# Moving the two halves of a split copy to other places in a software pipeline

## The chip, the core and the metric

The kernel runs on one core of a Trainium2 chip. The metric is device time in microseconds, the median of the runs shown. The engines named here are TensorE (PE in profiles, PEld for its weight loads), VectorE (DVE), ScalarE (ACT), GpSimd (POOL) and SyncE (SP, here the issuer of DMAs). Each works through its own queue in order, and semaphores tie them together.

## The reference

Four sequences of 1024 tokens with 128 features pass through an attention layer and a mixture-of-experts layer, each with a layer norm before, one behind and a residual. The change touches attention alone:

```python
q = (hidden_states @ Wq).reshape(b, s, H, D).transpose(0, 2, 1, 3)     # H 16, D 64
k = (hidden_states @ Wk).reshape(b, s, HKV, D).transpose(0, 2, 1, 3)   # HKV 4
v = (hidden_states @ Wv).reshape(b, s, HKV, D).transpose(0, 2, 1, 3)
q = _apply_rope(q, cos, sin)
k = _apply_rope(k, cos, sin)
scores = jnp.einsum('bkgqd,bkpd->bkgqp', qg, k) * scale
scores = jnp.where(causal, scores, jnp.float32(-1e+30))
probs = jax.nn.softmax(scores, axis=-1)
out = jnp.einsum('bkgqp,bkpd->bkgqd', probs, v)
```

## The kernel before, in words

Attention is one software pipeline of 128 steps: 4 batches (b), 4 key-value heads each (a "group", g), 8 steps a group (s, `STEPS_G`). A step treats two heads that share the partitions, and two tiles of 128 query rows: a big one, whose causal row has 1024, 896, 768 or 640 keys (steps 0 to 3, and again 4 to 7 for the second pair of heads), and a small one with 128, 256, 384 or 512 keys. The steps 2 to 7 of one group and 0 to 1 of the next stand in a hardware loop; the first two steps and the last six of a batch are written out.

Scores are made from operands in two parts, high and low, as q_high·k_high + q_low·k_high + q_high·k_low. Six "rope" tiles (k = 0 to 5, 128 x 512) supply them for each group: 0 and 1 are keys, 2 and 3 the queries of the first pair, 4 and 5 those of the second. `project_step(k)` says in which step a tile is projected: 0 to 3 in steps 3 to 6 of the group before, 4 and 5 in steps 0 and 1 of the group itself. A tile then passes through these stations:

- TensorE projects it into `proj_bank` at the end of its step; ScalarE's `keep_raw` (line 695) copies it to `raw`.
- SyncE's `swap_pairs` (line 315) moves neighbouring partitions of `raw` to `turned` with two DMAs.
- In the next step GpSimd multiplies `raw` by the cosines (line 927, after its own `spread_sums`, line 916), `turned` by the sines (line 907), and adds both into `roped` (line 932).
- In that next step too, ScalarE's `keep_high` (line 704) copies `roped` as float32r to the high tile, and VectorE's `rope_work(.., "low", ..)` (line 1038) subtracts that from `roped` into the low tile.

So a high copy is due in steps 4, 5, 6, 7, 1 and 2. The order of a step on each engine is fixed by the program:

- TensorE (`step`): big score rows (line 422, first the keys from 512 on, then the lower 512), which need the small exponentials of the step before for the lower part alone; three groups of transposes ("turns", line 441) of the last step's probabilities; the outputs of the step before that (line 471); small score rows, which need this step's big exponentials; two more groups of turns (441, 447); the projection.
- ScalarE (`step`): copy of the turned group 0 (line 725), two big exponentials (716), the high copy, two small exponentials, copy of the turned group 4, and `keep_raw`. At the end of a batch (`last`, s = 2) `keep_tokens` takes the next batch's tokens, at its start (s = 1) `keep_out` the projected output.
- VectorE (`attend`): reciprocal of the last step's sums (line 1052), two big maxima (1046), copies of the turned groups 1 and 2 (1060), the scaled output (1074), two small maxima, the turned group 3, the subtraction. In some steps of the first and last group parts of a layer norm follow (`next_norm`, `out_norm`).

GpSimd's spread waits for the reciprocal of the same step. Score rows wait for the low tiles (`rope_low`): big rows of step 0 for tile 2, small ones of step 0 for tile 3, big ones of step 4 for tile 5.

Of the kernel before, what the change touches and what calls it, by code (L numbers as in the profile page):

```python
# [13 lines left out]
B, S, HID = 4, 1024, 128  # L14
# [11 lines left out]
PROJ_A, PROJ_B = 4, 2  # L26
ROPES_G = PROJ_A + PROJ_B
ROPES_B = ROPES_G * HKV
STEPS_P = TILES // 2
STEPS_G = PAIRS * STEPS_P  # L30
# [14 lines left out]
def rope_index(b, g, k):  # L45

    return b * ROPES_B + g * ROPES_G + k


def step_index(b, g, s):  # L50

    return b * STEPS_B + g * STEPS_G + s


def widths(n):

    return n + 1, TILES - n
# [23 lines left out]
def half_of(k):  # L81

    return (0, 1, 1, 0, 1, 0)[k]


def project_step(k):

    return 3 + k if k < PROJ_A else k - PROJ_A
# [7 lines left out]
def rope_plan(b, s, lag, last):  # L96

    out = []
    for k in range(ROPES_G):
        if project_step(k) + lag == s and not (last and b == B - 1 and k < PROJ_A):  # L100
            out.append((1 if k < PROJ_A else 0, k))
    return out


def build(nc, io, out):
    with ExitStack() as ctx:
# [3 lines left out]
        def bank(name):  # L110
            return ctx.enter_context(nc.psum_tensor(name, [128, HALF], F32))
# [73 lines left out]
        o_out, proj_bank = bank("o_out"), bank("proj_bank")  # L185
# [47 lines left out]
        def earlier(g, s, lag):  # L233

            return (g, s - lag) if s >= lag else (g - 1, s - lag + STEPS_G)
# [130 lines left out]
        def _(pe):  # L366
# [108 lines left out]
            def step(b, g, s, last, depth):  # L475
# [29 lines left out]
                for ahead, k in rope_plan(b, s, 0, last):  # L505
                    project(b, g + ahead, k, proj_bank)
# [177 lines left out]
        def _(act):  # L684
# [12 lines left out]
            def keep_high(b, g, k):  # L697

                cols = slice(half_of(k) * HALF, half_of(k) * HALF + HALF)
                act.wait_ge(rope_sum, rope_index(b, g, k) + 1 + ROPES_G)  # L700
                if k < 2:
                    act.wait_ge(k_copied, 32 * (b * HKV + g + 1))
                dst = kk[0] if k < 2 else qh[0 if k < PROJ_A else 1]
                A(dst[:, cols], roped[:, k % 2, :], ACT.Copy).then_inc(rope_high, 1)  # L704

            def exponentials(b, g, s, big):

                n = s % STEPS_P
                sigma = step_index(b, g, s)
                width = widths(n)[big] * 128  # L710
                if big:
                    act.wait_ge(turn_full, MOVES * sigma + MOVES)
                for h in range(2):
                    item, q = (0 if big else 2) + h, block_at(n, big, h)
                    act.wait_ge(max_ready, 4 * sigma + item + 1)
                    A(probs[:, s % 2, q * 128:q * 128 + width], rows[h][:, 0:width], ACT.Exp,  # L716
                      bias=neg_max[:, s % 2, item:item + 1], accum_out=exp_sum[:, s % 2, item:item + 1]).then_inc(exp_done, 1)

            def keep_turned(b, g, s, j):

                sigma = step_index(b, g, s)
                first = moves(s % STEPS_P)[j][0]
                act.wait_ge(turn_full, MOVES * sigma + j + 1 + 2 * MOVES)
                act.wait_ge(pv_done, sigma + 1)
                A(probsT[:, s % 2, first * 128:first * 128 + HALF], ring[j % 3][:, :], ACT.Copy  # L725
                  ).then_inc(kept_act, 1)
# [8 lines left out]
            def keep_tokens(b, a, src):  # L735

                act.wait_ge(x_turned, 2 * b + a + 1)
                if b < B:
                    A(xT[:, 0, a * HALF:a * HALF + HALF], src[:, :], ACT.Copy).then_inc(x_high, 1)
                else:  # L740
                    A(x2T[a], src[:, :], ACT.Copy).then_inc(x2_kept, 1)

            def keep_out(b, a, src):

                act.wait_ge(wo_done, 2 * b + a + 1)
                if a == 0 and b:
                    act.wait_ge(mid_done, b)
                A(attn_out[:, 4 * a:4 * a + 4, :].rearrange("p t d -> p (t d)"), src[:, :], ACT.Copy).then_inc(wo_kept, 1)  # L748
# [8 lines left out]
            def step(b, g, s, last, depth):  # L757

                at = earlier(g, s, 1)
                first = isinstance(g, int) and g == 0  # L760
                if depth > 0:
                    keep_turned(b, *at, 0)
                exponentials(b, g, s, 1)
                for ahead, k in rope_plan(b, s, 1, last):
                    keep_high(b, g + ahead, k)
                if last and s == 2:
                    keep_tokens(b + 1, 0, proj_bank)
                if first and s == 1:
                    inverse_deviations(2 * b if b else 1, 0, TILES)
                if last and s == 4 and b:  # L770
                    inverse_deviations(2 * b + 1, TILES, 2 * TILES)
                exponentials(b, g, s, 0)
                if depth > 0:
                    keep_turned(b, *at, 4)
                if last and s == 2:
                    keep_tokens(b + 1, 1, proj_bank)
                if first and s == 1 and b:
                    keep_out(b - 1, 0, proj_bank)
                    keep_out(b - 1, 1, o_out)
                for ahead, k in rope_plan(b, s, 0, last):  # L780
                    keep_raw(b, g + ahead, k, proj_bank)
                if first and s == 0 and b:
                    keep_values(b)
# [157 lines left out]
        def _(dve):  # L941
# [80 lines left out]
            def rope_work(b, g, stage, k):  # L1022
                r, c = rope_index(b, g, k), k % 2
                cols = slice(half_of(k) * HALF, half_of(k) * HALF + HALF)
                if stage == "cos":
                    dve.wait_ge(rope_low, r + 1)
                    dve.wait_ge(raw_kept, r + 1)
                    V.tensor_tensor(roped[:, c, :], raw[:, k % 4, :], cf[:, C_COS + half_of(k) * HALF:C_COS + half_of(k) * HALF + HALF],
                                    ALU.mult).then_inc(cos_done, 1)
                elif stage == "sum":  # L1030
                    dve.wait_ge(cos_done, r + 1)
                    dve.wait_ge(sin_done, r + 1)
                    V.tensor_tensor(roped[:, c, :], roped[:, c, :], turned[:, c, :], ALU.add).then_inc(rope_sum, 1)
                else:
                    p = 0 if k < PROJ_A else 1
                    high, low = (kk[0], kl[0]) if k < 2 else (qh[p], ql[p])
                    dve.wait_ge(rope_high, r + 1)
                    V.tensor_tensor(low[:, cols], roped[:, c, :], high[:, cols], ALU.subtract).then_inc(rope_low, 1)

            def row_maxima(b, g, s, big):  # L1040

                width = widths(s % STEPS_P)[big] * 128
                for h in range(2):
                    item = (0 if big else 2) + h
                    dve.wait_ge(rows_full, 4 * step_index(b, g, s) + item + 1)
                    V.tensor_reduce(neg_max[:, s % 2, item:item + 1], rows[h][:, 0:width], AX_X, ALU.max, negate=True  # L1046
                                    ).then_inc(max_ready, 1)

            def invert_sums(b, g, s):

                dve.wait_ge(exp_done, 4 * step_index(b, g, s) + 8)
                V.reciprocal(inv_sum[:, s % 2, :], exp_sum[:, s % 2, :]).then_inc(sum_inverted, 1)  # L1052
# [23 lines left out]
            def attend(b, g, s, last, depth):  # L1076

                g1, s1 = earlier(g, s, 1)
                if depth > 0:
                    invert_sums(b, g1, s1)  # L1080
                row_maxima(b, g, s, 1)
                if depth > 0:
                    keep_turned(b, g1, s1, 1)
                    keep_turned(b, g1, s1, 2)
                if depth > 1:
                    keep_outputs(b, *earlier(g, s, 2))
                if last and s == 2 and b + 1 < B:
                    split_tokens(b + 1, 0, proj_bank)
                row_maxima(b, g, s, 0)
                if depth > 0:  # L1090
                    keep_turned(b, g1, s1, 3)
                for ahead, k in rope_plan(b, s, 1, last):
                    rope_work(b, g + ahead, "low", k)
                if last and s == 2 and b + 1 < B:
                    split_tokens(b + 1, 1, proj_bank)
                if isinstance(g, int) and g == 0 and s < 2:
                    next_norm(b, s)
                if last and b:
                    out_norm(b, s)
# [206 lines left out]
```

## Time and profile before

| | us |
|---|---|
| median of 3 runs | 1491.96 |
| lowest and highest | 1490.4, 1493.01 |
| the profiled execution | 1484.45 |
| its span, first to last instruction | 1482.4 |
| attention pipeline in it, roughly | 50 to 1156 |
| busy: TensorE, VectorE, ScalarE, GpSimd | 1333.7, 981.0, 774.2, 407.7 |

Busy time is a sum over stages. A matmul's end is modelled and overlaps the next one's start, so that a busy TensorE isn't one at its peak. Idle time is named in brackets with the instruction that ended it. An ordinary group of eight steps takes 63.8 us, and the groups at the ends of a batch take longer.

### The profile page before, as it was taken

Reading aid. Unit: us, or ns where it says so; the run is one execution under the profiler, and the core shown is the slowest. Engines: PE = TensorE matmul, PEld = TensorE weight load, DVE = VectorE, ACT = ScalarE, POOL = GpSimd, SP = SyncE. Lnnn points to the kernel's source line nnn. Section 1 sums busy time; section 2 is a strip of 40 time slices with the busy share of each in tenths; the row PEclk is TensorE's granted clock in tenths of the full one; section 3 lists DMA queues with packets and bytes.
Section 4 is the critical chain, followed back from the end, with each engine's and each line's share of the span. In section 5 each row is a group of like instructions: output and inputs, shape, how many; then the busy total and the mean of one; then the engine's idle time right before and its main releaser. Section 6 shows DMA issues by size and latency. Waiting matters only on the chain.

```text
span 1482.4 us, 31001 instructions
## 1 busy us (share of the span) xinstructions
PE 1333.7 (90%) x10417; PEld 931.1 (63%) x10432; DVE 981.0 (66%) x2044; ACT 774.2 (52%) x1709; POOL 407.7 (27%) x412
## 2 busy tenths in 40 slices
PE   2699999899999988998999989999999899999996
PEld 1477677677676766876766668676766644444442
DVE  3677777664777768476777775777768257666665
ACT  2556666554566556365566554666665233333333
POOL 0343444322434424143434331434440000000000
PEclk9799999999999999999999999999999999999999
DMA  8211112110111110112111111111110000000000
GB/s 235 82 38 64 60 46 67 38 58 28 64 53 67 35 61 29 58 41 69 35 67 57 43 54 33 55 50 67 49 57 2 1 1 8 7 8 8 8 8 14
DMA packets 79028, 67.64 MB, mean 46 GB/s; under 512 B 39904, under 2 KB 62304, under 8 KB 78816
## 3 DMA queue, kind: packets, MB, share of 16 engines
q1 hardware_dynamic: 78944, 66.55, 13.8%
q8 instruction: 49, 0.80, 0.2%
q14 instruction: 35, 0.29, 0.1%
HBM read 7.81 MB, written 2.10 MB: 7 GB/s over the span
## 4 chain that ended last, share of the span: by engine, by line
PE 36%; POOL 14%; ACT 14%; DMA 12%; issue 10%; DVE 7%; SPq 4%; ACTq 1%; POOLq 0%; DVEq 0%
DMA turned<-raw 12%; POOL turned L907 7%; POOL roped L932 7%; PE rows L611 7%; ACT probs L716 7%; PE rows L422 6%; PE o_out L471 5%; PE o_out L634 3%; PE turn L441 3%; ACT raw L695 3%; SPq L315 3%; ACT probsT L725 2%; DVE neg_max L1046 2%; PE o_out L390 2%; PE proj_bank L390 1%
## 5 line engine op out<-in xcount | busy, mean ns | idle before, releaser
L1046 DVE TENSOR_REDUCE neg_max<-rows 128x1 f32<-128x768 f32 (+7 forms) x512 | 363.7, 752 | 226.6 <-PE rows L425 226.6
L716 ACT ACTIVATE probs<-rows,neg_max 128x768 f32<-128x768 f32 (+7 forms) x512 | 373.2, 734 | 89.3 <-DVE neg_max L1046 86.2
L471 PE MATMUL o_out<-probsT,v_g 128*64 128x128 f32 (+1 forms) x3328 | 278.5, 318 | 0.7 <-DVE probsT L1060 0.7
L471 PEld LDWEIGHTS o_out<-probsT,v_g 128*64 128x64 f32 x3328 | 201.5, 137 | 68.5 <-issue 19.6
L441 PE MATMUL turn<-cf,probs 128*128 128x128 f32 x1792 | 242.8, 276 | 1.3 <-DVE probsT L1060 1.1
L422 PE MATMUL rows<-kk,qh 64*128 64x512 f32 (+2 forms) x768 | 170.8, 441 | 80.7 <-ACT probs L716 74.6
L725 ACT ACTIVATE probsT<-turn 128x512 f32<-128x512 f32 x256 | 152.5, 596 | 142.2 <-PE turn L441 138.4
L441 PEld LDWEIGHTS turn<-cf,probs 128*128 128x128 f32 x1792 | 195.1, 143 | 1.9 <-DVE probsT L1060 1.3
L916 POOL COPY inv_wide<-inv_sum 128x256 f32<-128x256 f32 x128 | 50.9, 398 | 507.3 <-DVE inv_sum L1052 476.5
L422 PEld LDWEIGHTS rows<-kk,qh 64*128 64x128 f32 x768 | 72.4, 185 | 168.2 <-ACT probs L716 120.3
L1060 DVE COPY probsT<-turn 128x512 f32<-128x512 f32 x256 | 174.5, 682 | 1.5 <-PE turn L441 1.1
L907 POOL TENSOR_TENSOR turned<-turned,cf 128x512 f32<-128x512 f32 x96 | 122.7, 1279 | 166.8 <-DMA turned<-raw 166.8
L611 PE MATMUL rows<-roped,w_exp 128*128 128x512 f32 x320 | 154.4, 606 | 1.1 <-ACT attn_out L748 0.7
L422 PE MATMUL rows<-kk,ql 64*128 64x512 f32 (+2 forms) x768 | 135.3, 348 | 0.0
L422 PE MATMUL rows<-kl,qh 64*128 64x512 f32 (+2 forms) x768 | 135.3, 347 | 0.0
L927 POOL TENSOR_TENSOR roped<-raw,cf 128x512 f32<-128x512 f32 x92 | 117.2, 1274 | 55.3 <-ACT raw L695 55.2
L932 POOL TENSOR_TENSOR roped<-roped,turned 128x512 f32<-128x512 f32 x92 | 117.2, 1274 | 13.3
L1174 DVE TENSOR_TENSOR probs<-rows,probs 128x512 f32<-128x512 f32 x80 | 55.1, 688 | 90.7 <-PE o_out L634 76.1
L704 ACT ACTIVATE qh<-roped 128x512 fp32r<-128x512 f32 x64 | 40.4, 631 | 133.7 <-POOL roped L932 132.4
L860 ACT ACTIVATE probs<-rows 128x512 f32<-128x512 f32 x80 | 47.8, 597 | 102.5 <-PE rows L611 102.4
L716 ACT ACTIVATION_READ_ACCUMULATOR probs<-rows,neg_max 128x1 f32 x512 | 100.9, 197 | 0.0
L611 PEld LDWEIGHTS rows<-roped,w_exp 128*128 128x128 f32 x320 | 59.9, 193 | 64.5 <-issue 58.7
(154 smaller groups left out, 1677.8 us busy)
## 6 DMA issues: line engine op xcount, KB each, us to landing
turned<-raw SPq DMA_DIRECT2D x192, 128.0 KB, 2.0
kk<-kk SPq DMA_DIRECT2D x16, 512.0 KB, 2.9
kl<-kl SPq DMA_DIRECT2D x16, 512.0 KB, 3.7
v_g<-v_all SPq DMA_DIRECT2D x32, 256.0 KB, 3.0
slab_a<-w_qk SPq DMA_DIRECT2D x16, 256.0 KB, 2.6
xm<-in_x SPq DMA_DIRECT2D x4, 512.0 KB, 7.4
slab_b<-w_qk SPq DMA_DIRECT2D x16, 128.0 KB, 2.2
out<-xm SPq DMA_DIRECT2D x8, 256.0 KB, 2.3
```

Of the source, the lines that this page charges most:

```text
L422: mm(rows[h][:, first:end], q[p][half, tile:tile + 128], k[p][half, first:end], start=n_pass == 0, stop=n_pass == 2 and not first <= tile ...
L441: ins = nc.tensor.transpose(ring[j % 3][:, (q - first) * 128:(q - first) * 128 + 128], probs[:, s % 2, q * 128:q * 128 + 128], ident)
L471: ins = mm(dst, v_g[p][:, t, :], x, start=t == 0, stop=t == big_w - 1)
L611: ins = mm(dst[:, :], w_exp[:, part, items[i], :], h1T[n % 2], start=True, stop=True)
L716: A(probs[:, s % 2, q * 128:q * 128 + width], rows[h][:, 0:width], ACT.Exp, bias=neg_max[:, s % 2, item:item + 1], accum_out=exp_sum[:, s ...
L725: A(probsT[:, s % 2, first * 128:first * 128 + HALF], ring[j % 3][:, :], ACT.Copy).then_inc(kept_act, 1)
L907: P.tensor_tensor(turned[:, c, :], turned[:, c, :], cf[:, C_SIN + half_of(k) * HALF:C_SIN + half_of(k) * HALF + HALF], ALU.mult).then_inc( ...
L927: P.tensor_tensor(roped[:, c, :], raw[:, k % 4, :], cf[:, C_COS + half_of(k) * HALF:C_COS + half_of(k) * HALF + HALF], ALU.mult).then_inc( ...
L932: P.tensor_tensor(roped[:, c, :], roped[:, c, :], turned[:, c, :], ALU.add).then_inc(rope_sum, 1)
L1046: V.tensor_reduce(neg_max[:, s % 2, item:item + 1], rows[h][:, 0:width], AX_X, ALU.max, negate=True).then_inc(max_ready, 1)
L1060: V.tensor_copy(probsT[:, s % 2, first * 128:first * 128 + HALF], ring[j % 3][:, :]).then_inc(kept_dve, 1)
L1174: V.tensor_tensor(guT[q % 2], up_u[q % 2][:, :], gT[q % 2], ALU.mult).then_inc(ex_gu, 1)
```

## The change

ScalarE: `keep_high` no longer stands between the big and the small exponentials. It comes behind the small ones, the copy of the turned group 4 and `keep_out`, and ahead of `keep_tokens` of the second half and of `keep_raw`. VectorE: the subtraction is taken from the end of the step (after the turned group 3) to the next step, between the reciprocal and the big maxima. `low_plan` says which tile is due: that whose projection was two steps ago, tile 3 thus in step 0 of its own group. Nothing is computed otherwise, no semaphore is added, and the start of the kernel (tiles 0 to 3 of the first group) stays as it was.

```diff
@@ -99,6 +99,18 @@
     for k in range(ROPES_G):
         if project_step(k) + lag == s and not (last and b == B - 1 and k < PROJ_A):
             out.append((1 if k < PROJ_A else 0, k))
+    return out
+
+
+def low_plan(b, g, s, last):
+
+    out = []
+    for k in range(ROPES_G):
+        at = project_step(k) + 2
+        if at == s and not (last and b == B - 1 and k < PROJ_A):
+            out.append((b, g + 1 if k < PROJ_A else g, k))
+        if at == s + STEPS_G and not (b == 0 and isinstance(g, int) and g == 0):
+            out.append((b, g, k))
     return out
 
 
@@ -761,8 +773,6 @@
                 if depth > 0:
                     keep_turned(b, *at, 0)
                 exponentials(b, g, s, 1)
-                for ahead, k in rope_plan(b, s, 1, last):
-                    keep_high(b, g + ahead, k)
                 if last and s == 2:
                     keep_tokens(b + 1, 0, proj_bank)
                 if first and s == 1:
@@ -772,11 +782,13 @@
                 exponentials(b, g, s, 0)
                 if depth > 0:
                     keep_turned(b, *at, 4)
-                if last and s == 2:
-                    keep_tokens(b + 1, 1, proj_bank)
                 if first and s == 1 and b:
                     keep_out(b - 1, 0, proj_bank)
                     keep_out(b - 1, 1, o_out)
+                for ahead, k in rope_plan(b, s, 1, last):
+                    keep_high(b, g + ahead, k)
+                if last and s == 2:
+                    keep_tokens(b + 1, 1, proj_bank)
                 for ahead, k in rope_plan(b, s, 0, last):
                     keep_raw(b, g + ahead, k, proj_bank)
                 if first and s == 0 and b:
@@ -1078,6 +1090,8 @@
                 g1, s1 = earlier(g, s, 1)
                 if depth > 0:
                     invert_sums(b, g1, s1)
+                for b0, g0, k in low_plan(b, g, s, last):
+                    rope_work(b0, g0, "low", k)
                 row_maxima(b, g, s, 1)
                 if depth > 0:
                     keep_turned(b, g1, s1, 1)
@@ -1089,8 +1103,6 @@
                 row_maxima(b, g, s, 0)
                 if depth > 0:
                     keep_turned(b, g1, s1, 3)
-                for ahead, k in rope_plan(b, s, 1, last):
-                    rope_work(b, g + ahead, "low", k)
                 if last and s == 2 and b + 1 < B:
                     split_tokens(b + 1, 1, proj_bank)
                 if isinstance(g, int) and g == 0 and s < 2:
```

## Rows read from the trace of the kernel before

**Rows 1.** The page's chain that ended last, by line

```profile
DMA turned<-raw 12%; POOL turned L907 7%; POOL roped L932 7%; PE rows L611 7%; ACT probs L716 7%; PE rows L422 6%; PE o_out L471 5%; PE o_out L634 3%; PE turn L441 3%; ACT raw L695 3%; SPq L315 3%; ACT probsT L725 2%; DVE neg_max L1046 2%; PE o_out L390 2%; PE proj_bank L390 1%
```

**Rows 2.** Waits of the whole span: who for whom, us, times, longest

```profile
ACT qh L704 <- POOL roped L932: 132.4, 59, 4.3
...
PE rows L422 <- ACT probs L716: 74.6, 101, 3.8
```

**Rows 3.** Busy time of each engine in one group: stretch, length, engines, clock

```profile
464.95:528.79 63.84, 60.11 (x564) 44.84 (x564) 45.95 (x78) 39.23 (x93) 26.12 (x26) 1.00 0.16 55
```

**Rows 4.** Timeline, ScalarE and GpSimd, steps 1 to 3: start, us, what

```profile
473.14 0.60 ACT L695 ACTIVATE raw<-proj_bank 128x512 f32<-128x512 f32 x1
...
473.89 1.27 POOL L927 TENSOR_TENSOR roped<-raw,cf 128x512 f32<-128x512 f32 x1 [0.25 <-ACT raw L695]
476.51 1.28 POOL L907 TENSOR_TENSOR turned<-turned,cf 128x512 f32<-128x512 f32 x1 [1.35 <-DMA turned<-raw]
477.93 1.27 POOL L932 TENSOR_TENSOR roped<-roped,turned 128x512 f32<-128x512 f32 x1
...
479.23 0.63 ACT L704 ACTIVATE qh<-roped 128x512 fp32r<-128x512 f32 x1 [2.31 <-POOL roped L932]
479.77 0.56 ACT L716 ACTIVATE probs<-rows,neg_max 128x384 f32<-128x384 f32 x1
...
480.88 0.59 ACT L725 ACTIVATE probsT<-turn 128x512 f32<-128x512 f32 x1
...
481.44 0.40 POOL L916 COPY inv_wide<-inv_sum 128x256 f32<-128x256 f32 x1 [2.25 <-DVE inv_sum L1052]
...
484.71 0.21 ACT L716 ACTIVATION_READ_ACCUMULATOR probs<-rows,neg_max 128x1 f32 x1
```

**Rows 5.** Timeline, VectorE, the same stretch

```profile
478.36 1.02 DVE L1046 TENSOR_REDUCE neg_max<-rows 128x1 f32<-128x384 f32 x2 [0.33 <-PE rows L425]
...
479.90 0.69 DVE L1038 TENSOR_TENSOR ql<-roped,qh 128x512 fp32r<-128x512 f32 x1
...
482.20 1.56 DVE L1046 TENSOR_REDUCE neg_max<-rows 128x1 f32<-128x640 f32 x2 [1.00 <-PE rows L425]
```

**Rows 6.** Timeline, TensorE: score rows of steps 3, 6, 7 and 0

```profile
479.19 0.39 PE L422 MATMUL rows<-kk,qh 64*128 64x256 f32 x2
...
481.04 0.50 PE L422 MATMUL rows<-kk,qh 64*128 64x512 f32 x2 [1.23 <-ACT probs L716]
...
485.57 0.51 PE L422 MATMUL rows<-kk,qh 64*128 64x512 f32 x2
...
504.88 0.50 PE L422 MATMUL rows<-kk,qh 64*128 64x512 f32 x2 [0.53 <-ACT probs L716]
...
513.17 0.50 PE L422 MATMUL rows<-kk,qh 64*128 64x512 f32 x2 [0.60 <-ACT probs L716]
...
521.61 0.51 PE L422 MATMUL rows<-kk,qh 64*128 64x512 f32 x2 [0.95 <-ACT probs L716]
...
526.43 0.38 PE L422 MATMUL rows<-kk,qh 64*128 64x256 f32 x2 [0.21 <-ACT probs L716]
```

**Rows 7.** Timeline, VectorE and ScalarE, step 7 and the next step 0

```profile
518.87 1.29 DVE L1046 TENSOR_REDUCE neg_max<-rows 128x1 f32<-128x512 f32 x2 [0.51 <-PE rows L425]
...
520.13 0.67 ACT L716 ACTIVATE probs<-rows,neg_max 128x512 f32<-128x512 f32 x1
...
522.79 2.35 DVE L1046 TENSOR_REDUCE neg_max<-rows 128x1 f32<-128x1024 f32 x2 [1.02 <-PE rows L425]
```

**Rows 8.** Timeline, VectorE and GpSimd at the kernel's start

```profile
39.12 1.29 DVE L1028 TENSOR_TENSOR roped<-raw,cf 128x512 f32<-128x512 f32 x2
...
39.85 1.69 POOL L907 TENSOR_TENSOR turned<-turned,cf 128x512 f32<-128x512 f32 x1 [3.18 <-DMA turned<-raw]
```

**Rows 9.** Timeline: end of batch 1, step 2; a late swap in batch 3

```profile
546.92 0.63 PE L383 MATMUL proj_bank<-cf,x_norm 128*128 128x128 f32 x4 [3.31 <-issue]
...
946.65 1.28 POOL L907 TENSOR_TENSOR turned<-turned,cf 128x512 f32<-128x512 f32 x1 [2.50 <-DMA turned<-raw]
```

## Prediction

> **What bounds the kernel now.** I read first the chain of work that ended last. It doesn't hang on one engine: beside TensorE it runs through the transfer that swaps the pairs of a rope tile, through GpSimd's products, and through ScalarE [rows 1]. Then the waits: ScalarE sits still 132.4 us, in 59 places, before its copy of a rotated q tile, for GpSimd's sum (the k tiles come on top); and TensorE sits still 74.6 us before score rows for ScalarE's exponentials [rows 2]. In the third view, the windows, I take one ordinary group of eight steps (batch 1, group 2): 63.84 us, of which TensorE is busy 60.11 [rows 3]. So TensorE is the floor, and 3.7 us of a group are open to a better order.
>
> The timeline shows where these lie. Around step 2 [rows 4]: raw copy 473.14, swap, GpSimd's products and the sum until 479.20, high copy 479.23, small exponentials from 479.77, copy of turned probabilities 480.88. VectorE's small maxima began at 478.36; the first of the pair is done by 478.91 [rows 5]. So the exponentials wait 0.85 us behind a copy that they don't need. TensorE has begun the upper part of the next big rows at 479.19 and stands before the lower part until 481.04, the moment at which the small exponentials end [rows 6]. Its steps with a high copy are thus tied to a ring: raw, swap, three GpSimd operations, high copy, exponentials, turned copy, next raw: about 8 us, against 7.5 us of TensorE's work a step. The stalls before the lower part are shown as idle 1.23, 0.53, 0.60 and 0.95 us (ahead of the big rows of steps 3, 6, 7 and of the next 0) [rows 6]; the last matmul recorded before each overlaps by 0.17, so I price them 1.40, 0.70, 0.77 and 1.12. This pattern repeats in nearly all groups.
>
> **The change, part by part.** Nothing is added or removed: the same 92 loop copies and 92 subtractions run, in other places.
>
> *ScalarE's copy goes behind the small exponentials and the turned copy.* The exponentials start when the first maximum is there. Gain at each stall, the smaller of the shift and of the stall:
> - step 2 to 3: shift 479.77 - 478.91 = 0.86 of 1.40: 0.86 [rows 4, 5, 6]
> - step 5 to 6: its copy has 0.63 + waiting, and the maxima are ready over 1 us before; all 0.70 [rows 6]
> - step 6 to 7: likewise all 0.77 [rows 6]
> - step 7 to 0: maxima from 518.87, the first done at 519.56; exponentials began 520.13: 0.57 of 1.12 [rows 6, 7]
>
> Does the copy's new place hold anything? It sits ahead of this step's raw copy. In the frame of step 2: exponentials end 480.1, turned copy to 480.6 (an operation follows a copy at 0.5), high 480.6 to 481.3. Where a raw copy follows it ends about 0.6 later, 1.7 us after the exponentials; the third group of turns, which needs that bank, begins only after the next big rows and two groups of turns, some 2.5 us after TensorE's step begins. Nothing on TensorE waits. GpSimd's sum is in time too: raw copy's end 473.74 to the sum's end 479.20 is 5.46 us [rows 4]; a step is then 7.4 us and more, so the sum is there 0.7 to 2 us before ScalarE comes to it. The ring is now 5.5 + 0.6 + 0.6 = 6.7 us and no longer binds. A swap that lands late (GpSimd idle 2.50 instead of 1.35 before the product [rows 9]; the trace has 13 over 1.7 us, together about 12 us over the usual) is today a longer stall, and is then mostly absorbed: I take 4 of 12 us.
>
> *VectorE's subtraction goes ahead of the next step's big maxima.* It takes 0.69 [rows 5], starts when the high copy ends, and the next operation can follow after about 0.61. Where the rows are full before that, the maxima are late:
> - step 3: high ends 481.27, subtraction 481.3, maxima 481.9. The lower part starts at 480.20 and the rows are full 1.16 later (today 481.04 to 482.20), at 481.36. Late by 0.55. But today the big exponentials end at 484.92 and TensorE comes back to small rows at 485.57: 0.65 of cover [rows 4, 5, 6]. Cost nothing, but the cover is all used: 0.5 more would be paid.
> - steps 2, 5 and 6: the small exponentials before are short, so late by 0 to 0.1. Nothing.
> - step 7: late by about 0.4, same widths as step 3, same cover. Nothing.
> - step 0: widest maxima, and TensorE already waits here for big exponentials (0.21 [rows 6]): no cover. Exponentials of step 7 end 519.60 + 1.43 = 521.03, turned copy to 521.5, high to 522.14, subtraction 522.18, maxima 522.79: exactly when they start today [rows 7]. The 0.57 gained ahead is handed back.
>
> Sum for an ordinary group: 0.86 + 0.70 + 0.77 + 0 = 2.3 us. Fifteen groups (the last of batch 3 has no tiles for a next one) give 35. To this: at the end of a batch, step 2, ScalarE's copy of the next batch's tokens stood behind the high copy. TensorE is idle 3.31 us there in batch 1 [rows 9], the largest of four, 6.6 together; with the 0.86 counted already, I take 4 more. Late swaps 4. Against it: in those last groups VectorE has a batch's norm to do behind the step, and then the subtraction ahead of maxima (about 0.6 to 1 us in three steps of three batches, bound 0 to 8): 3. Net 35 + 4 + 4 - 3 = 40 us. Bounds: from 24 (step 3 and 7 pay, extras nothing) to 55 (all 3.7 us of idle of each of 15 groups).
>
> *One resource that the move touches.* VectorE's subtraction reads two tiles in SBUF, GpSimd's products too. The start of the kernel has the only rows where such operations overlap: a GpSimd product started at 39.85, while a VectorE product of two SBUF tiles ran to 40.41, and took 1.69 us; a loop one takes 1.28 [rows 8, 4]. So they exclude each other for about the time of the overlap. Today the subtraction runs while GpSimd is idle. Moved, it starts 1.15 after the exponentials' end; GpSimd's spreading copy lies at 0.46 to 0.86 after it (from the row of step 2: reciprocal, then spread), and the cos product starts 0.15 after the raw copy's end, at about 1.77, the subtraction ending at 1.84. The two miss each other but for 0.1 us, and the subtraction is first. Cost nothing by this.
>
> The Trainium skill, page SBUF — State Buffer, section Who interferes with whom, speaks against the move here: a VectorE instruction with two SBUF inputs and a GpSimd instruction that reads SBUF use one port pair, and the second to issue is blocked until the first ends. The stretched product in the trace agrees with it (+0.41 us). What it would make of the time is the slower rival.
>
> **The rivals.**
> - *The subtraction in front of the maxima is paid for in full.* If the cover at steps 3 and 7 isn't there (copy or subtraction 0.3 later than worked out), steps 3, 7, 6 and 2 pay 0.55 + 0.4 + 0.1 + 0.1 = 1.15 a group; 17 us less: gain 23 to 27, 1467. For it: only 0.1 us of cover is left at step 3.
> - *More is gained.* If the step 0 stall shrinks as well and late swaps vanish, nearly all idle of the groups goes: 15 x 3.7 = 55 us, 1437. For it: a stall in one step lets the next ones slip in the ring; against it: step 0's arithmetic, and exponentials of width 512 that end after the upper part in any order.
> - *Nothing moves:* ScalarE would have to wait for GpSimd's sum at the new place as long as at the old one. The sum would have to be 1.5 us later than its 5.46; no stretch of the loop shows that often. 1489 to 1495.
> - *Slower: subtraction behind the cos product.* If GpSimd's cos product starts first, the subtraction waits for its 1.28 us and ends at 1.77 + 1.28 + 0.69 = 3.7 after the exponentials instead of 1.84. That happens from the point where VectorE is more than 0.6 us late at the copy's end. It concerns four of a group's six subtractions (in steps 2, 5, 6, 7: there a raw copy followed the high copy in the step before); beyond the cover each loses about 1.4: 5.5 against 2.3 gained, 3.2 x 15 = 48 us slower, 1540. Against it: the high copy ends before the raw copy, and VectorE has nothing else to do then.
>
> **How the numbers follow.** The profiled execution took 1484.45 us (span 1482.4), the median of the runs is 1491.96, 0.5% above it. 40 us off the profiled one is 1444.5; off the median 1452, which I give. Chances: forecast 0.62, paid in full 0.17, more gained 0.12, nothing 0.03, slower 0.06. The range takes in the second and the third case: 1436 to 1470. About 0.2% (3 us) is what a measurement can tell from no change: faster 0.91, same 0.03, slower 0.06.
>
> **What would show it.** In the changed profile: ScalarE's wait for GpSimd's sum nearly gone; small exponentials 0.3 to 0.7 us after the small maxima start in every step; no idle TensorE before the lower parts of steps 6 and 7, about 0.4 left at 3 and 0; at step 0 big maxima right behind the subtraction, and more idle before its small rows (0.7 to 0.9 instead of 0.21); an ordinary group of 61.5 us. Wrong would be: GpSimd's or VectorE's two-input operations longer than 1.28 and 0.69, the sum late at the copy's new place, or big exponentials of steps 3 and 7 ending after TensorE's outputs.

## The result and the profile after

| us | before | after |
|---|---|---|
| median (4 runs each) | 1492.49 | 1429.21 |
| lowest to highest | 1490.4 to 1494.42 | 1428.56 to 1429.99 |
| the profiled execution | 1484.45 | 1428.59 |
| its span | 1482.4 | 1426.5 |

The ratio of after to before is 0.9577, with a 95% interval of 0.956 to 0.9593. The direction was right and the size wrong: 63 us less on the median against 40 forecast, and 1429 lies below the range of 1436 to 1470.

The chain that ended last has changed its nature. By engine and by line (the page's view), after:

```profile
PE 66%; DVE 12%; issue 9%; ACT 8%; SPq 2%; DMA 2%; POOL 1%; DVEq 0%; ACTq 0%; POOLq 0%
PE rows L434 15%; PE o_out L483 12%; PE turn L453 8%; PE rows L623 7%; DVE neg_max L1058 5%; ACT probs L728 4%; PE o_out L646 3%; PE rows L437 3%; PE proj_bank L453 3%; PE o_out L402 2%; PE proj_bank L402 2%; DMA turned<-raw 1%; PE proj_bank L385 1%; PE proj_bank L387 1%; PE proj_bank L386 1%
```

In before the swap and GpSimd's two lines held a quarter of it [rows 1]; now transfers (DMA) and GpSimd hold 3% together, and TensorE 66%. In the waits of the whole span, after, ScalarE's wait for GpSimd's sum [rows 2] is in no row any more; VectorE's wait for the high copy has come instead:

```profile
DVE ql L1050 <- ACT qh L716: 82.0, 56, 12.1
...
PE rows L434 <- ACT probs L728: 42.6, 74, 3.8
```

TensorE's wait for exponentials fell from 74.6 to 42.6 us. The timeline around steps 2 and 3 of batch 1, group 2, after, answers to [rows 4 to 6]:

```profile
457.16 1.27 POOL L944 TENSOR_TENSOR roped<-roped,turned 128x512 f32<-128x512 f32 x1
...
457.41 1.02 DVE L1058 TENSOR_REDUCE neg_max<-rows 128x1 f32<-128x384 f32 x2 [0.33 <-PE rows L437]
...
458.00 0.58 ACT L728 ACTIVATE probs<-rows,neg_max 128x384 f32<-128x384 f32 x1 [2.02 <-DVE neg_max L1058]
...
459.13 0.60 ACT L737 ACTIVATE probsT<-turn 128x512 f32<-128x512 f32 x1
459.61 0.64 ACT L716 ACTIVATE qh<-roped 128x512 fp32r<-128x512 f32 x1
...
460.28 0.69 DVE L1050 TENSOR_TENSOR ql<-roped,qh 128x512 fp32r<-128x512 f32 x1 [0.83 <-ACT qh L716]
460.89 1.55 DVE L1058 TENSOR_REDUCE neg_max<-rows 128x1 f32<-128x640 f32 x2
...
463.20 0.20 ACT L728 ACTIVATION_READ_ACCUMULATOR probs<-rows,neg_max 128x1 f32 x1
```

The exponentials start 0.59 us behind the start of their maxima (1.41 in before), the high copy 0.48 behind the turned copy, the subtraction 0.67 later, the maxima 0.61 behind that. The sum ended at 458.43, 1.18 us before its copy. On TensorE:

```profile
459.29 0.50 PE L434 MATMUL rows<-kk,qh 64*128 64x512 f32 x2 [0.42 <-ACT probs L728]
...
463.82 0.49 PE L434 MATMUL rows<-kk,qh 64*128 64x512 f32 x2
...
496.11 0.50 PE L434 MATMUL rows<-kk,qh 64*128 64x512 f32 x2
...
497.51 0.50 PE L434 MATMUL rows<-kk,qh 64*128 64x512 f32 x2 [0.43 <-ACT probs L728]
...
502.75 0.38 PE L434 MATMUL rows<-kk,qh 64*128 64x256 f32 x2 [0.64 <-ACT probs L728]
```

The stalls ahead of steps 6 and 7 are gone; those ahead of 3 and 0 are 0.42 and 0.43; before step 0's small rows it grew to 0.64 from 0.21 [rows 6]. The group's row in the windows view, after, against [rows 3]:

```profile
436.52:497.51 60.99, 59.28 (x562) 44.74 (x563) 45.66 (x79) 39.47 (x93) 26.15 (x26) 1.00 0.17 58
```

The group takes 60.99 instead of 63.84, 2.85 less; and TensorE's busy time for the same matmuls fell as well, from 60.11 to 59.28, at a granted clock of 1.00 in both.

### The profile page after: what moved, and what is told of

It is laid out like the page before. It is cut to its first block, busy times and chain, and to the rows that moved or that the text cites. A ratio compares the mean times of both kernels' runs of the same rounds, so it can differ in the third digit from the quotient of the medians.

```text
span 1426.5 us, 31016 instructions
## 1 busy us (share of the span) xinstructions
PE 1316.9 (92%) x10432; PEld 925.0 (65%) x10432; DVE 978.3 (69%) x2044; ACT 778.0 (55%) x1709; POOL 409.5 (29%) x412
## 4 chain that ended last, share of the span: by engine, by line
PE 66%; DVE 12%; issue 9%; ACT 8%; SPq 2%; DMA 2%; POOL 1%; DVEq 0%; ACTq 0%; POOLq 0%
PE rows L434 15%; PE o_out L483 12%; PE turn L453 8%; PE rows L623 7%; DVE neg_max L1058 5%; ACT probs L728 4%; PE o_out L646 3%; PE rows L437 3%; PE proj_bank L453 3%; PE o_out L402 2%; PE proj_bank L402 2%; DMA turned<-raw 1%; PE proj_bank L385 1%; PE proj_bank L387 1%; PE proj_bank L386 1%
## 5 line engine op out<-in xcount | busy, mean ns | idle before, releaser
L453 PE MATMUL turn<-cf,probs 128*128 128x128 f32 x1792 | 239.5, 274 | 1.3 <-DVE probsT L1072 1.1
L434 PE MATMUL rows<-kk,qh 64*128 64x512 f32 (+2 forms) x768 | 164.8, 425 | 48.1 <-ACT probs L728 42.6
L453 PEld LDWEIGHTS turn<-cf,probs 128*128 128x128 f32 x1792 | 192.2, 141 | 1.9 <-DVE probsT L1072 1.3
L623 PEld LDWEIGHTS rows<-roped,w_exp 128*128 128x128 f32 x320 | 59.2, 191 | 63.8 <-issue 58.0
L1050 DVE TENSOR_TENSOR ql<-roped,qh 128x512 fp32r<-128x512 f32 x64 | 44.0, 689 | 82.1 <-ACT qh L716 82.0
```

Source lines behind the costliest of these rows:

```text
L434: mm(rows[h][:, first:end], q[p][half, tile:tile + 128], k[p][half, first:end], start=n_pass == 0, stop=n_pass == 2 and not first <= tile ...
L453: ins = nc.tensor.transpose(ring[j % 3][:, (q - first) * 128:(q - first) * 128 + 128], probs[:, s % 2, q * 128:q * 128 + 128], ident)
L623: ins = mm(dst[:, :], w_exp[:, part, items[i], :], h1T[n % 2], start=True, stop=True)
```

## The experiments

Three theories stood against each other. A: the gain is the ring's, opened by ScalarE's part; what my sum lacked are waits hidden in TensorE's busy time, late swaps and batch ends. B: VectorE's part carries a share of its own. C: ordinary groups vary from execution to execution. The experiments ran on three chips, and the median of before was 1490.76 us on the first (13 runs), 1490.95 on the second (13) and 1487.49 on the third (7). The changed kernel was not run beside them, so a difference from its 1429.21 goes across chips; the times of single groups, read from the traces, carry such comparisons.

### Before once more

> The kernel before, unchanged, profiled once more. The profiled execution of before took 1484.45 us and the median of its runs 1492; for the changed kernel both are 1429. Theory A: the executions of before differ in how many swaps land late (13 with over 1.7 us of wait in the first trace, ordinary 1.38), since each late swap lengthens the ring and the changed kernel has slack for it. An execution of 1490 us should then show about 6 us more in late swaps and TensorE stalls behind them, ordinary groups staying at 63.8 us. Theory B: ordinary groups themselves vary, and 63.8 becomes 64.2.

Measured: 1493.58 us, 9.1 more than the first profiled execution; ordinary groups again 63.8 to 63.9. GpSimd's waits for the swap, first the row of the first execution, then that of this one (us, times, longest):

```profile
POOL turned L907 <- DMA turned<-raw: 166.8, 90, 33.7
```

```profile
POOL turned L907 <- DMA turned<-raw: 171.3, 89, 34.1
```

Summed over single waits above 1.7 us, what exceeds the usual 1.38 is 11.9 us in the first and 16.9 in the second; three groups with late swaps (the first of batches 0, 1 and 3) make up 9.0 us of the difference. So C falls: executions of before differ at late swaps. But 5 us more of lateness went with 9 us more of time. Part of the rest shows in the granted clock. Inside the attention pipeline it fell from 1.00 to 0.5 (from 2.4 to 1.2 GHz), for 3.4 us each time, four times in the first execution (at 292, 548, 593 and 678 us) and eight times in this one, five of them in the three groups named; what one fall costs is measured below. The trace that I predicted from was one of the quickest executions of before: 1484.45 against a median of 1492.

### One half of the change at a time

VectorE's part alone: the changed kernel with ScalarE's copy back in its old place.

```diff
                 exponentials(b, g, s, 1)
+                for ahead, k in rope_plan(b, s, 1, last):
+                    keep_high(b, g + ahead, k)
...
-                for ahead, k in rope_plan(b, s, 1, last):
-                    keep_high(b, g + ahead, k)
                 if last and s == 2:
                     keep_tokens(b + 1, 1, proj_bank)
```

> ScalarE's copy stays between the big and the small exponentials; VectorE's subtraction is moved behind the reciprocal as in the changed kernel. Theory A: nothing is gained, 1489 to 1496, the exponentials still stand behind the copy. Rival (VectorE's part carries some of the gain that my sum missed): 1470 to 1485.

Measured: 1491.36 us, ratio 1.0009 (0.9994 to 1.0023). By itself VectorE's part gives nothing, and B falls in that form; what it is worth beside ScalarE's part is the next question.

ScalarE's part alone: the subtraction back at the end of its step.

```diff
-                for b0, g0, k in low_plan(b, g, s, last):
-                    rope_work(b0, g0, "low", k)
                 row_maxima(b, g, s, 1)
...
                     keep_turned(b, g1, s1, 3)
+                for ahead, k in rope_plan(b, s, 1, last):
+                    rope_work(b, g + ahead, "low", k)
```

> ScalarE's copy behind the small exponentials as in the changed kernel; VectorE's subtraction stays at the end of its step, thus ahead of the reciprocal. Theory A (the gain is ScalarE's part alone, since the ring no longer goes through the copy): 1429 to 1436, the reciprocal's 0.2 us being added before the big maxima of step 0. Rival (the subtraction must be moved as well, since it holds reciprocal and spread): the spread comes 1.5 us later and GpSimd's sum with it, the ring is back in part: 1450 or more.

Measured: 1442.24 us, ratio 0.9673 (0.9655 to 0.9691): between the two expectations. Ordinary groups take 61.0 us as in the changed kernel, so ScalarE's part gives all of their gain, and the rival's late spread costs nothing there. But the pipeline ends 12.4 us later than in the changed kernel. Some 10 of that lie in the last group of a batch and the first of the next; 2.5 lie in the kernel's first group, where TensorE's granted clock was 0.5 for 7 us of this execution against 1 us; after_late and low_after_max show that too, so it isn't this kernel's own. VectorE's timeline in batch 1, group 0, at the end of step 1, in this kernel:

```profile
331.85 0.69 DVE L1050 TENSOR_TENSOR ql<-roped,qh 128x512 fp32r<-128x512 f32 x1 [15.02 <-ACT qh L716]
332.46 0.15 DVE L985 TENSOR_TENSOR newton<-rstd 128x8 f32<-128x8 f32 x1
...
333.26 2.14 DVE L992 TENSOR_SCALAR x_norm<-xm,mean_var,rstd 128x128 f32<-128x128 f32 x8
335.32 0.17 DVE L1064 RECIPROCAL inv_sum<-exp_sum 128x4 f32<-128x4 f32 x1
335.41 0.93 DVE L1058 TENSOR_REDUCE neg_max<-rows 128x1 f32<-128x768 f32 x1
```

The subtraction waits 15.02 us at the head of the queue, since the high copy now stands behind `keep_out`, which waits for TensorE's projected output; the layer norm that could have filled the time runs after it, and the next maxima start 3.56 us behind the subtraction. In the changed kernel the norm is done during the wait:

```profile
329.56 0.69 DVE L1050 TENSOR_TENSOR ql<-roped,qh 128x512 fp32r<-128x512 f32 x1 [12.07 <-ACT qh L716]
330.79 0.96 DVE L1058 TENSOR_REDUCE neg_max<-rows 128x1 f32<-128x768 f32 x1 [0.54 <-PE rows L437]
```

To test that cause alone, the same kernel with the subtraction behind the norms:

```diff
                     keep_turned(b, g1, s1, 3)
-                for ahead, k in rope_plan(b, s, 1, last):
-                    rope_work(b, g + ahead, "low", k)
...
                 if last and b:
                     out_norm(b, s)
+                for ahead, k in rope_plan(b, s, 1, last):
+                    rope_work(b, g + ahead, "low", k)
```

> ScalarE's part of the change alone, as in act_only, with the subtraction behind the pieces of the layer norms and the second half of the tokens instead of ahead of them. In act_only ordinary groups took 61.0 us as in the changed kernel, and it lost 12.5 us at batch ends: in step 1 of a batch's first group the subtraction stood 15.02 us at the head of VectorE's queue, behind ScalarE's keep_out, with the layer norm and the reciprocal behind it. Theory A: with the norm ahead, 6 us or more come back, 1430 to 1436. Rival (what is lost there is the reciprocal's and the spread's lateness): 1440 or more.

Measured: 1430.13 us, within 1 us of the changed kernel's 1429.21; all of the 12 us are back, and group for group its trace lies within 0.5 us of the changed kernel's. So all that VectorE's part does is to keep the norms from standing behind the subtraction.

### Does the ring bind, and what is its slack?

> The kernel before with one more GpSimd copy (128 x 256, about 0.40 us, into a tile that nobody reads) between the sine product and the sum of each tile. Theory A (the ring binds in before): up to six rounds a group pay about 0.43 us each: 20 to 40 us slower than before, 1512 to 1532. Rival (TensorE binds and the stalls have another cause): within 5 us of before.

> The changed kernel with the same extra GpSimd copy. Theory A (the ring has 0.7 us and more of slack now): within 3 us of the changed kernel, 1428 to 1432. Rival (the ring still binds in some steps): 10 us or more slower.

The edit in both:

```diff
                     sin_product(b, g + ahead, k)
+                    P.tensor_copy(idle_tile[:], cf[:, C_COS:C_COS + 256])
                     pool.wait_ge(cos_done, r + 1)
```

Measured: before with the copy 1508.32 us (1.0143, 1.0099 to 1.0186), 17 more; after with the copy 1428.95, nothing. (One of the four runs with the copy took 1517.74; without it the median is 1505.75, 15 more.) The ring binds in before, but the first bound of 20 was missed, because the copy costs the ring less than it takes. GpSimd's timeline, before with the copy:

```profile
508.93 1.27 POOL L908 TENSOR_TENSOR turned<-turned,cf 128x512 f32<-128x512 f32 x1 [1.37 <-DMA turned<-raw]
510.14 0.40 POOL L931 COPY idle_tile<-cf 128x256 f32<-128x256 f32 x1
510.50 1.27 POOL L934 TENSOR_TENSOR roped<-roped,turned 128x512 f32<-128x512 f32 x1
```

The sum starts 1.57 behind the sine product instead of 1.42 [rows 4]: the copy fills the gap in which the sum waited for its semaphores. 0.15 in each of six rounds is 0.9 a group, and the groups grew from 63.8 to 64.8: every round pays in full.

A lateness of the size of a late swap, for tile 1 alone:

```diff
                     sin_product(b, g + ahead, k)
+                    if k == 1:
+                        P.tensor_tensor(idle_tile[:], cf[:, C_SIN:C_SIN + HALF], cf[:, C_COS:C_COS + HALF], ALU.mult)
                     pool.wait_ge(cos_done, r + 1)
```

> The kernel before, with one GpSimd product more (128 x 512, 1.27 us, into a tile that nobody reads) between the sine product and the sum of tile 1 alone: once a group the sum comes about 1.1 us late, as behind a late swap (the gap of 0.14 us between product and sum is filled first, as the extra copy of 0.40 us showed, which lengthened the ring by 0.15). Theory A (the ring binds, so that a late sum is paid for in full): 15 x 1.1 = 17 us slower than before, 1506 to 1510. Rival (late sums are partly caught up by TensorE's idle time in other steps): 5 to 10 us.

> The changed kernel with the same late sum of tile 1. Theory A (the sum has some 1 us of slack before the copy's new place, and the maxima 0.4 behind it): 0 to 3 us slower than the changed kernel, 1429 to 1432. Rival (late swaps aren't absorbed, they were only rarer in the trace): 17 us slower, 1446.

Measured: 1505.01 us against 1487.49 for before (1.0107, 1.0063 to 1.015), 17.5 more as expected, and 1431.66 with the change, 2.5 more than the changed kernel. Ordinary groups went from 63.8 to 64.9 and stayed at 61.0. A sum that is 1.1 us late is paid for in full in before; with the change it costs ordinary groups nothing, and the whole kernel about a seventh as much. Late swaps make the sum late in the same way, and the changed kernel hides them too: its own trace has 15.4 us of lateness over the usual and act_norm_first's 6.6, and the two profiled executions took 1428.59 and 1428.37 us.

The first of these two kernels also shows what a fall of the clock costs. Two of its ordinary groups, alike but for the clock (the windows view; the clock is the third number from the end):

```profile
123.81:189.42 65.61, 61.34 (x565) 45.95 (x564) 45.94 (x78) 39.38 (x93) 27.31 (x27) 0.97 0.16 54
189.42:254.36 64.94, 60.12 (x564) 44.84 (x563) 45.99 (x78) 39.26 (x93) 27.35 (x27) 1.00 0.16 55
```

TensorE in step 6 of the first and of the second:

```profile
164.80 0.50 PE L423 MATMUL rows<-kk,qh 64*128 64x512 f32 x2 [1.60 <-ACT probs L717]
...
166.09 1.91 PE L442 MATMUL turn<-cf,probs 128*128 128x128 f32 x8
...
230.46 0.50 PE L423 MATMUL rows<-kk,qh 64*128 64x512 f32 x2 [1.57 <-ACT probs L717]
...
231.48 1.04 PE L442 MATMUL turn<-cf,probs 128*128 128x128 f32 x8
```

After nearly the same idle time the clock fell in one group and not in the other; eight transposes then took 1.91 us instead of 1.04, step 6 was 1.58 us longer, and step 7 gave 0.89 back. A fall thus cost 0.7 us here; where nothing gives time back I estimate 1.7, half of its 3.4. In the traces of before such falls stand behind the long stalls of TensorE (1.67 to 3.3 us of idle time in the first). The changed kernel's trace has none inside the pipeline once its first steps are through.

### What the subtraction costs in front of the maxima

The subtraction is made twice in every step (`times` is 2 there), the first time into a tile that nobody reads:

```diff
                     dve.wait_ge(rope_high, r + 1)
+                    for _ in range(times - 1):
+                        V.tensor_tensor(idle_tile[:], roped[:, c, :], high[:, cols], ALU.subtract)
                     V.tensor_tensor(low[:, cols], roped[:, c, :], high[:, cols], ALU.subtract).then_inc(rope_low, 1)
```

> The changed kernel with a second subtraction (into a tile that nobody reads) ahead of the one that counts, so that the big maxima start 0.61 us later. Theory A (the maxima have about 0.4 us of cover left in steps 2, 3, 5, 6, 7 and none in step 0): 0.61 + five times 0.2 = 1.6 us a group, 26 us slower than the changed kernel, 1450 to 1460. The second subtraction now falls beside GpSimd's cos product (four steps of a group). If they exclude each other and GpSimd's product is first, each of the four pays some 1.3 us more: 1530. If the subtraction is first, only the product is late, and it stays at 1455. Rival (the maxima have cover everywhere): 1430.

Measured: 1458.99 us, 29.8 more than the changed kernel. Ordinary groups: 62.5, 1.5 more; step 0 pays 0.60 and the steps 2, 3, 6 and 7 0.21 to 0.23, step 5 0.07. The cover is as worked out. The rest of the loss, some 7 us, lies in the groups at batch ends. The second subtraction now meets GpSimd's cosine product:

```profile
464.99 0.69 DVE L1052 TENSOR_TENSOR idle_tile<-roped,qh 128x512 f32<-128x512 f32 x1 [0.83 <-ACT qh L717]
465.60 0.69 DVE L1053 TENSOR_TENSOR ql<-roped,qh 128x512 fp32r<-128x512 f32 x1
```

```profile
465.59 1.83 POOL L940 TENSOR_TENSOR roped<-raw,cf 128x512 f32<-128x512 f32 x1 [0.77 <-ACT raw L708]
```

The product takes 1.83 us instead of 1.27, and the subtraction its usual 0.69: GpSimd is the one that waits, and has slack for it. At two batch ends the product started first, and there the subtraction paid, 1.76 us instead of 0.69, with the maxima behind it:

```profile
562.11 1.40 POOL L940 TENSOR_TENSOR roped<-raw,cf 128x512 f32<-128x512 f32 x1 [0.28 <-ACT raw L708]
562.30 1.76 DVE L1053 TENSOR_TENSOR kl<-roped,kk 128x512 fp32r<-128x512 f32 x1
```

That is the mechanism of the slower rival. In the changed kernel itself the order was never so; at the same two batch ends (546 and 814 us) the subtraction came first, and took 0.86, with the product at 1.40 and 1.41.

So the subtraction should stand where nothing queues for it, behind the big maxima:

```diff
-                for b0, g0, k in low_plan(b, g, s, last):
-                    rope_work(b0, g0, "low", k)
                 row_maxima(b, g, s, 1)
+                for b0, g0, k in low_plan(b, g, s, last):
+                    rope_work(b0, g0, "low", k)
```

> The changed kernel with the subtraction behind the big maxima instead of ahead of them. Theory A: the 0.64 us of idle TensorE before the small rows of step 0 fall to the 0.21 of before (15 times), other steps have cover for either order: 6 to 8 us less than the changed kernel, 1421 to 1424. Rival: the later copies of turned groups 1 and 2 hold TensorE, or the low tile 3 comes late for step 0's small rows: 1429 or more.

Measured: 1420.65 us, ratio to before 0.9525 (0.9509 to 0.9541), 8.6 less than the changed kernel and the best version here. Ordinary groups take 60.5 instead of 61.0, all of it in step 0 (8.56 instead of 8.99), and the idle time before step 0's small rows is 0.21 again.

### Batch ends

The kernel before, with the first half of the next batch's tokens copied ahead of the high copy in step 2 of a batch's last group:

```diff
-                for ahead, k in rope_plan(b, s, 1, last):
-                    keep_high(b, g + ahead, k)
                 if last and s == 2:
                     keep_tokens(b + 1, 0, proj_bank)
+                for ahead, k in rope_plan(b, s, 1, last):
+                    keep_high(b, g + ahead, k)
```

> The kernel before with one change: at the end of a batch, step 2, ScalarE's copy of the next batch's tokens goes ahead of the high copy instead of behind it. Theory A: of the 6.6 us that TensorE is idle there in four batches some 5 go, 1487 against 1492. Rival (the small exponentials still stand behind the high copy, and take it back): under 2 us.

Measured: 1483.29 us, 7.7 less than before (0.9949, 0.9926 to 0.9973). The tokens' stall was real, and worth at least what I took for it. In the trace the steps 2 of the last groups of batches 0, 1 and 2, counted from the lower part of the big rows to the next lower part, went from 10.00, 11.95 and 9.99 us to 8.28, 9.98 and 8.29, 5.4 us in all; runs of this kernel scatter from 1477 to 1492, so that the remaining 2 us mean little.

## Why the prediction was right or wrong

The direction and the mechanism came true. What failed is the sum: it gave 40 us, and the gain on the medians is 63.3. Of the 23.3 us that it lacked, 7.5 belong to the term of the ordinary group, 6.9 to the terms of late swaps and batch ends, 7.4 to the choice of the execution it was taken from, and 1.5 to what lies outside the attention pipeline (behind it the trace of before has one fall of the clock more, 3.4 us long).

- **The bound and the mechanism: right.** TensorE stood behind exponentials that stood behind the high copy. The extra copy and the late sum showed the ring, and moving ScalarE's copy alone gave ordinary groups their whole gain.
- **The order of events: right to 0.1 us.** Predicted for step 3, in the frame of before: stall of 0.6 left, high copy 0.5 behind the turned one, maxima 0.55 late, covered. Measured: lower part 1.05 behind the upper (0.46 in step 2, without stall), so 0.59 left, and the maxima directly behind the subtraction with no idle TensorE after the outputs. For step 0: maxima "exactly when they start today" relative to the upper rows: 3.00 us behind them here (499.11 - 496.11), 3.09 in before. What was gained ahead was handed back, as written. Only the idle time before step 0's small rows came out a little below the 0.7 to 0.9 expected, at 0.64.
- **Term "ordinary group 2.3 us": too small by 0.5, 7.5 us in all. This is the step whose failure the runs show best.** I took the stalls that the trace shows as idle. Starts of big rows give each step's length:

| step | 1 | 2 | 3 | 4 | 5 | 6 | 7 | 0 | sum |
|---|---|---|---|---|---|---|---|---|---|
| before | 7.41 | 6.83 | 9.08 | 7.85 | 7.61 | 8.21 | 7.76 | 9.09 | 63.84 |
| after | 7.41 | 6.72 | 8.28 | 7.87 | 7.42 | 7.42 | 6.88 | 8.99 | 60.99 |

  Steps 3, 6 and 7 gave 0.80, 0.79 and 0.88 against 0.86, 0.70 and 0.77. Step 0 gave 0.10, where I had nothing: its idle time went from 0.95 + 0.21 to 0.43 + 0.64. Steps 2 and 5 gave 0.11 and 0.19, and for them the timeline of before names no idle time. Their waits show as a record that is longer. The first matmuls of the lower part in step 2, before and after:

```profile
472.82 0.50 PE L422 MATMUL rows<-kk,qh 64*128 64x512 f32 x2
```

```profile
451.98 0.40 PE L434 MATMUL rows<-kk,qh 64*128 64x512 f32 x2
```

  So busy time of the same work fell by 0.83 us a group, beside 2.02 of idle time. My sum saw the idle time and an overlap of 0.17 at four stalls, and nothing of steps 2 and 5.
- **Term "late swaps 4 of 12 us": wrong, all of them.** I had named the mechanism and then took a third without a reason. The late sum costs before 17.5 and after 2.5 us. With 12 us of lateness in the execution that I took, and nearly all of it hidden by the change, this term was up to 8 us too small. It also lacked the clock: two of the four falls in the pipeline of before (292 and 678 us) stand behind a late swap. At 0.7 to 1.7 us each, an estimate from before_late, the four falls cost 3 to 7 us, of which the changed kernel pays nothing.
- **Reference execution: taken as typical, and it wasn't.** I subtracted from the median what I had worked out in an execution 7.5 us below it. Both numbers were at hand. In before_again, the one slower execution with a trace, the difference lay at late swaps and the clock falls near them, which the change takes away. The gain between the profiled executions is 55.9 us, between the medians 63.3.
- **Term "batch ends +4, -3": the cost didn't come.** The norms did not delay the subtraction: it was the other way, and VectorE's part prevents just that (act_only against act_norm_first, 12 us). Attention became 54.4 us shorter between the two profiled executions; 15 ordinary gains of 2.83 are 42.5, and 11.9 remain for late swaps, batch ends and the falls of the clock together, where I had 5. The eight groups in the middle of batches gave 24.0 (2.8 to 2.9 each, and 4.2 in one with a late swap), the eight at batch ends 30.4. How much of that is a late swap's, the tokens' or the clock's can't be told from these two executions.
- **The slower rival: its condition did not come about in the changed kernel, but its rule holds.** The two engines do hold each other up in operations that read two SBUF tiles: in double_low the product took 1.83 instead of 1.27 us where it was second, and the subtraction 1.76 instead of 0.69 where that was. The Trainium skill (page SBUF — State Buffer, section Who interferes with whom) says that a VectorE instruction with two SBUF inputs contends with a GpSimd instruction that reads SBUF. The trace agrees, in both orders. In the change the subtraction comes first by 0.6 us (452.51 and 453.11 in step 2), and the overlap of 0.09 us stretched nothing. Even a doubled subtraction made mostly GpSimd lose, which is the harmless side.
- **The range: too narrow below.** The rival "more is gained" was priced at all idle time of the groups, 55 us, as though idle time were all that can be gained; late swaps, clock and busy time came on top.

## What to carry to other kernels

Price a stall by the length of the step from one start to the next, and look at whether busy time can shrink too; the idle time shown is a lower bound. When a ring through several engines is opened, everything late in it is hidden at once, late transfers included, so compare the profiled execution with the median before subtracting. Look at the granted clock of each group too: a long stall of TensorE can cost more than its own length. An instruction that waits long belongs behind work that is ready, in every queue: moving one engine's copy late made the other engine's subtraction hold up a layer norm for 15 us.

## What the runs showed of the hardware

A 0.40 us GpSimd copy put between a product and the sum that waits for it lengthened the chain by 0.15 us: the sum starts 1.42 us behind the product's start without it and 1.57 with it, though the product alone takes 1.27 us. A swap of pairs, two DMAs, kept GpSimd waiting over 1.7 us (1.37 as a rule in before) in 8 to 13 of some 87 cases in every trace. They are not spread at random: all lie in the first or the last group of a batch, but for one place early in group 1 of batch 2. What makes them late was not tried. Between a VectorE subtraction and a GpSimd product, both with two SBUF inputs, the product lost 0.56 us where the two started together, and the subtraction 1.07 where the product had started 0.19 us before it. TensorE's granted clock fell from 1.00 to 0.5 for 3.4 us behind idle times of 1.60 and 1.57 us in ordinary groups of before_late, and stayed at 1.00 behind another 1.57; the fall cost 0.7 us in the group.
